# A graph layer on one core: group 0 worked in pairs of tiles, the row table moved to step 3, and five unused matmuls at TensorE's start

## The reference

```
h = relu(layernorm(x))                            # per node
W_rel = einsum('rb,bdf->rdf', w_comp, weight)     # 32 types from 8 bases
agg[type, dst] += h[src] * norm                   # per edge
node = einsum('rnd,rdf->nf', agg, W_rel) + bias + h @ loop_weight
out = x + relu(node)
```

## Time and profile before

| | |
|---|---|
| median of 3 runs | 1015.2 us (1015.01 to 1015.9) |
| the profiled execution | 1015.24 us, its span 1013.5 us |
| TensorE busy | 990.3 us, 98% |
| VectorE busy | 955.0 us, 94% |
| ScalarE busy | 884.6 us, 87% |
| GpSimd busy | 723.8 us, 71% |
| granted TensorE clock, mean | 0.999 |

### The profile page before, as it was taken

One profiled execution on the slowest core, in us unless ns is written; L12 is line 12 of the kernel. 1 busy time (PEld: TensorE's weight loads), 2 busy tenths in 40 slices (PEclk: granted clock), 3 DMA queues, 4 the chain that ended last, 5 costly groups with the idle time before them and its releaser, 6 DMA issues.

```text
span 1013.5 us, 23775 instructions
## 1 busy us (share of the span) xinstructions
PE 990.3 (98%) x4902; PEld 574.4 (57%) x4902; DVE 955.0 (94%) x4366; ACT 884.6 (87%) x3242; POOL 723.8 (71%) x1282
## 2 busy tenths in 40 slices
PE   5899999999999999999999999999999999999996
PEld 2355555555556565656565555555555655555655
DVE  6999999999999999999999999999999999999995
ACT  6898989898888889898989898989898988889884
POOL 6877777777777777777777777777777777777740
PEclk9999999999999999999999999999999999999999
DMA  4556555556556555565565555465655655555544
GB/s 116 145 135 165 149 156 164 156 144 169 143 152 173 140 154 161 152 166 155 143 173 141 154 162 158 138 178 140 168 152 152 166 148 155 159 155 141 156 123 140
DMA packets 178223, 154.47 MB, mean 152 GB/s; under 512 B 17781, under 2 KB 151213, under 8 KB 178077
## 3 DMA queue, kind: packets, MB, share of 16 engines
q1 hardware_dynamic: 157261, 101.40, 35.6%
q0 software_dynamic: 20384, 51.32, 19.7%
q10 hardware_dynamic: 432, 0.22, 0.1%
HBM read 101.31 MB, written 51.56 MB: 151 GB/s over the span
## 4 chain that ended last, share of the span: by engine, by line
PE 93%; DVE 2%; POOL 2%; issue 1%; ACT 1%; DMA 1%; DVEq 0%; ACTq 0%; POOLq 0%
PE y_ps L790 33%; PE y_ps L797 31%; PE win_ps L812 9%; PE win_ps L807 8%; PE hT_ps L876 4%; PE hT_ps L803 4%; PE mix_ps L868 1%; POOL xg L578 1%; DVE sum_a L1019 1%; DVE sum_b L1019 0%; DMA xg<-x,idx 0%; DVE msg L1052 0%; PE y_ps L812 0%; DMA src_all<-src 0%; PE y_ps L807 0%
## 5 line engine op out<-in xcount | busy, mean ns | idle before, releaser
L578 POOL DMA_INDIRECT xg<-x,idx x392 | 382.0, 974 | 73.4 <-issue 34.0
L790 PE MATMUL y_ps<-w_all,hT 128*128 128x512 f32 x784 | 412.3, 608 | 2.9 <-DVE sum_a L1019 2.7
L797 PE MATMUL y_ps<-w_all,hT 128*128 128x512 f32 x784 | 400.3, 592 | 0.0
L523 POOL TENSOR_TENSOR u<-z 128x128 f32<-128x128 f32 x392 | 180.4, 460 | 182.8 <-ACT z L626 178.9
L626 ACT ACTIVATE z<-y_ps,mix 128x128 f32<-128x128 f32 x784 | 244.5, 366 | 44.8 <-PE y_ps L797 37.8
L1019 DVE SCALAR_TENSOR_TENSOR sum_b<-y_ps,mix,sum_b 128x128 f32<-128x128 f32 x784 | 265.8, 339 | 0.0
L797 PEld LDWEIGHTS y_ps<-w_all,hT 128*128 128x128 f32 x784 | 149.1, 190 | 187.9 <-issue 164.0
L790 PEld LDWEIGHTS y_ps<-w_all,hT 128*128 128x128 f32 x784 | 132.3, 189 | 119.1 <-DVE sum_a L1019 60.9
L622 ACT ACTIVATE z<-y_ps,mix 128x128 f32<-128x128 f32 x392 | 140.8, 359 | 63.6 <-issue 44.9
L660 ACT ACTIVATE hw<-xw,shift,nrstd 128x128 f32<-128x128 f32 x391 | 192.6, 494 | 0.4 <-DVE shift L1121 0.4
L1019 DVE SCALAR_TENSOR_TENSOR sum_b<-y_ps,mix,z 128x128 f32<-128x128 f32 x392 | 131.4, 335 | 36.1 <-issue 32.3
(11 more groups left out here) (107 smaller groups left out, 1174.3 us busy)
## 6 DMA issues: line engine op xcount, KB each, us to landing
seg<-msgs SPq DMA_DIRECT2D x391, 104.8 KB
msgs<-msg SPq DMA_DIRECT2D x98, 258.0 KB
xw<-x POOLq DMA_DIRECT2D x97, 256.0 KB
out<-res SPq DMA_DIRECT2D x97, 256.0 KB
xg<-x,idx POOLq DMA_INDIRECT x392
type_bc<-type_rows SPq DMA_DIRECT2D x52, 112.0 KB
w_all<-weight SPq DMA_DIRECT2D x1, 512.0 KB
type_bc<-type_rows SPq DMA_DIRECT2D x4, 80.0 KB
```

Of the source, the lines that this page charges most:

```text
L523: nc.gpsimd.tensor_tensor(u[:, r, :], z[:, r, 0, :], z[:, r, 1, :], ALU.add).then_inc(s_u, 1)
L578: nc.gpsimd.indirect_dma_start(xg[:, q, j, :], None, x, bass.IndirectOffsetOnAxis(ap=idx[:, q, j:j + 1], axis=0)).then_inc(s_gather[q * G ...
L790: nc.tensor.matmul(y_ps[2 * t % 5][:, :, :], hT[:, q, j, :], w_all[:, B // 2:B, :], start=True, stop=True).then_inc(s_y_high, 1)
L797: nc.tensor.matmul(y_ps[(2 * t + 1) % 5][:, :, :], hT[:, q, j, :], w_all[:, 0:B // 2, :], start=True, stop=True).then_inc(s_y, 1)
```

## The change

In group 0 each tile gets its own `neg_mean`; tiles 0 and 1 are transposed and copied to `hT` by themselves (`first_tiles`), and the products of tile 0 stand ahead of the transposes of tiles 2 and 3, those of tile 1 behind them. `w_all` is loaded straight behind the first types, and the rest of `src_all` behind the fourth gather. Of the 8 `sign` instructions four are moved into ScalarE's steps 1 and 2. `bin_counts(0)` moves to the start of VectorE's step 1, `bin_counts(1)` to the start of its step 3 and `row_table` to the end of that step; the 8 matmuls of `count_bins` stand together in TensorE's step 3. Five matmuls 128x384 in float32 into bank `y_ps[4]`, whose result nothing reads, stand ahead of the first mixing matmul.

```diff
+TABLE_STEP = 3
+PAIR = 2
...
@@ SyncE
-            sp.dma_start(src_all[:, FIRST:NT], src[:, FIRST:NT]).then_inc(s_src, 16)
-            sp.wait_ge(s_gather[1], 16)
             sp.dma_start(w_all[:, :, :], weight.rearrange("b d f -> d b f")).then_inc(s_all, 16)
             sp.wait_ge(s_gather[G - 1], 16)
+            sp.dma_start(src_all[:, FIRST:NT], src[:, FIRST:NT]).then_inc(s_src, 16)
@@ ScalarE, step: behind mixing(1) i = 0, behind mixing(3) i = 1
+                def late_sign(i):
+                    if is_before(g, TABLE_STEP):
+                        sign(SPAN // 2 + 2 * (g - 1) + i)
@@ ScalarE, group 0
-            for k in range(SPAN - 2):
+            for k in range(SPAN // 2 - 1):
                 sign(k)
...
+            for j in range(PAIR):
+                act.wait_ge(s_mean_first, j + 1)
+                first_relu(j)
+            act.wait_ge(s_hT_first, 1)
+            nc.scalar.activation(hT[:, 0, 0:PAIR, :], hT_ps[:, 0:PAIR, :], ACT.Copy).then_inc(s_hT_sb_first, 1)
+            sign(SPAN // 2 - 1)
+            act.wait_ge(s_mean_first, PAIR + 1)
+            first_relu(PAIR)
             act.wait_ge(s_mean, 1)
-            first_relu(2)
-            first_relu(3)
+            first_relu(G - 1)
@@ TensorE
+            pe.wait_ge(s_step, 2)
+            for k in range(5):
+                nc.tensor.matmul(y_ps[4][:, 0:3, :], ident[:, :], win_off[:, 0:3 * P], start=True, stop=True)
...
                 messages(0)
                 messages(1)
+                if g == TABLE_STEP:
+                    count_bins()
...
+            def first_tiles():
+                for j in range(PAIR):
+                    pe.wait_ge(s_relu, j + 1)
+                    mm = nc.tensor.transpose(hT_ps[:, j, :], h[:, 0, j, :], ident[:, :])
+                mm.then_inc(s_hT_first, 1)
+                pe.wait_ge(s_hT_sb_first, 1)
+                pe.wait_ge(s_all, 16)
+                product_high(0, 0, 0)
+                product_low(0, 0, 0)
+                for j in range(PAIR, G):
+                    pe.wait_ge(s_relu, j + 1)
+                    mm = nc.tensor.transpose(hT_ps[:, j, :], h[:, 0, j, :], ident[:, :])
+                mm.then_inc(s_hT, 1)
+                product_high(0, 0, 1)
+                product_low(0, 0, 1)
@@ VectorE, step
+                if g == 1:
+                    bin_counts(0)
+                if g == TABLE_STEP:
+                    bin_counts(1)
                 tile_slot(g, n, q, 0, more)
...
                 tile_slot(g, n, q, 3, False)
                 stats_of(3)
+                if g == TABLE_STEP:
+                    row_table()
                 if more:
                     one_hot(g + 1, (q + 1) % RING)
@@ VectorE, group 0
+                dve.wait_ge(done, 2 * (j % DV) + 2)
+                nc.vector.tensor_scalar(neg_mean[:, 0, j:j + 1], nmv[:, NRING - 1, j, 0:1], -1.0, None,
+                                        ALU.mult).then_inc(s_mean_first if j < G - 1 else s_mean, 1)
                 if j == 1:
...
                     one_hot(0, 0)
-                    bin_counts(0)
...
-            bin_counts(1)
             step(0, 0, 0)
-            row_table()
```

More of the change, by code:

```diff
@@ L270, in build_layer @@
         s_mean_first = sem("s_mean_first")
+        s_hT_first = sem("s_hT_first")
+        s_hT_sb_first = sem("s_hT_sb_first")
         s_dst = sem("s_dst")
@@ L627, in scale_bases, with sign @@
                 ins.then_inc(s_z, 1)
+            def sign(k):
+                nc.scalar.activation(signs[:, k, :], dst_f[:, :], ACT.Sign, bias=limits[:, k:k + 1], scale=-1.0,
+                                     accum_out=below_sum[:, k:k + 1]).then_inc(s_below, 1)
             def group_means(g, n, q):
@@ L704, in step @@
                 mixing(1)
+                late_sign(0)
                 if here:
@@ L719, in step @@
                 mixing(3)
+                late_sign(1)
                 if not beyond(g, NG - 1):
@@ L729, in _ @@
             act.wait_ge(s_limits, 1)
[L730 to L732 removed]
             def first_relu(j):
                 nc.scalar.activation(h[:, 0, j, :], xg[:, 0, j, :], ACT.Relu, bias=neg_mean[:, 0, j:j + 1]).then_inc(s_relu, 1)
[L737 removed]
+            for k in range(SPAN // 2 - 1):
                 sign(k)
[L739 to L743, removed]
+            for j in range(PAIR):
[6 more added lines that the diff above has]
+            first_relu(PAIR)
             act.wait_ge(s_mean, 1)
[L745 to L746 removed]
+            first_relu(G - 1)
             nc.scalar.activation(std[:, 0, :], nmv[:, NRING - 1, :, 1], ACT.Sqrt, bias=eps_col[:, 0:1]).then_inc(s_std, 1)
             act.wait_ge(s_hT, 1)
[L749 removed]
+            nc.scalar.activation(hT[:, 0, PAIR:G, :], hT_ps[:, PAIR:G, :], ACT.Copy).then_inc(s_hT_sb, 1)
             group_means(1, 0, 1)
@@ L772, in _, with count_bins @@
         def _(pe):
-            def count_bins(half):
+            def count_bins():
                 counts = win_ps[0:1, :, :].rearrange("p b f -> p (b f)")
                 pe.wait_ge(s_first_hot, 1)
-                pe.wait_ge(s_bins, half + 1)
-                for k in range(half * (SPAN // 2), (half + 1) * (SPAN // 2)):
+                pe.wait_ge(s_bins, 2)
+                for k in range(SPAN):
                     mm = nc.tensor.matmul(counts[:, 0:BINS], in_bin16[:, k:k + 1], first_hot[:, SPAN - k:SPAN - k + BINS],
                                           start=k == 0, stop=k == SPAN - 1)
-                if half == 1:
-                    mm.then_inc(s_hist, 1)
+                mm.then_inc(s_hist, 1)
+            pe.wait_ge(s_step, 2)
+            for k in range(5):
+                nc.tensor.matmul(y_ps[4][:, 0:3, :], ident[:, :], win_off[:, 0:3 * P], start=True, stop=True)
             pe.wait_ge(s_weights, 16)
@@ L840, in messages @@
                 def messages(j):
-                    if 1 <= g <= NG:
-                        if j == 0:
+                    if 1 <= g <= NG and not (is_before(g, 2) and j < PAIR):
+                        if j == (PAIR if is_before(g, 2) else 0):
                             pe.wait_ge(s_hT_sb, g)
-                        if g == 1 and j == 0:
-                            pe.wait_ge(s_all, 16)
                         product_high(g - 1, (q - 1) % RING, j)
@@ L870, in step @@
                     if is_before(g, 1):
-                        count_bins(0)
+                        first_tiles()
+                        return
                     pe.wait_ge(s_relu, g * G + G)
```

6 lines of the change are left out of this document (removed).

## The result

Ten executions of each, taken in turn on one chip: before 1015.62 us (1015.01 to 1016.89), after 1018.44 us (1017.65 to 1020.11). The ratio is 1.0029 with an interval of 1.0020 to 1.0038, some 2.8 us, above the forecast of 1016.8 and just above the range. The profiled execution of after took 1018.74 us with a span of 1017.0 (before 1015.24 and 1013.5).

A forecast was written before the change was run, and what follows sets the result against it. TensorE bounds the full pipeline; GpSimd's first `u` and VectorE from 32 us decide its gap-free start. +2.49 + 0.34 - 1.2 = +1.6 us on a profiled 1015.24, median 1016.8; range 1014.6 to 1018.3.

The forecast's parts named there:

- The table: VectorE's step 3: row table 2.49 us plus `bin_counts(1)` 0.34, taken as the full 2.83 us of cost; bounds 0 and 2.83.
- The first `u`: GpSimd's first `u`, 20.26 us before: expected 1.2 us earlier, bounds 0.34 and 1.48, passed whole to VectorE at 32.26.
- case B: Slower: constant loads in the DMA queue keep group 1's last gather late; 1017.7, or 1019.2 at worst; chance 0.30.
- The bins on TensorE: Eight small matmuls in TensorE's step 3, beside the row table's time: zero, up to 1.46 us if uncovered.
- the signs: Four signs moved into gaps of ScalarE's steps 1 and 2: zero, 0.60 us without that cover.
- the five unused matmuls: TensorE, ahead of the first mixing matmul: can give back 0.90 us of the first product, which has slack: zero.
- The head start of the first products: TensorE's first product near 10.7 us instead of 16.74; TensorE must then wait, any gain read at GpSimd's `u`.
- Case E: Faster: TensorE's products start 6.0 us earlier and GpSimd does not hold that gain back; 1012.0; chance 0.10.
- C: VectorE's lateness in step 3 is made good before TensorE's gaps end, so the table is covered; 1014.0; chance 0.08.
- D: TensorE's first product was on the path and its clock counts: 0.9 less than forecast, 1015.9; chance 0.07.

## Why the prediction was wrong

**The table: right in place and size.** 2.49 and 0.34, together 2.83 us, were to go over whole to the product of tile 14. That product is 2.94 us late with `u` unmoved, and with `u` 1.9 us earlier it is 1.93 us less late. The last matmul moved by 2.84, and the kernel with the table back at the start gives 3.1.

**The first `u`: the step that failed.** The sum took off 1.2 us, "near the upper end, because both parts of that wait are relieved"; its bounds were 0.34 and 1.48. Measured: 0.02 later in the profile of after, and 0.23 and 0.30 earlier (20.03 and 19.96) in two kernels with the same loads, without the unused matmuls and with the gap filled, in which GpSimd began on time. The text looked at one road, ScalarE's: its new loads "are what the last gather of group 1 competes with". That gather did stay late. But the lower bound held GpSimd's gain at 14.89 or better, and in front of the gain stands a gather too, the sixth, issued at 11.27 beside loads issued from 11.13 on. The gain came at 16.12, and at 15.87 and 15.80 in those two kernels. With the constant loads out of its way the reward came: 1.9 us at the first `u`, more than the upper bound. The mechanism is that of case B, which was to decide once `u` came after 19.46; its price of 1017.7 still held 0.34 us of gain, and with that at zero the sum is 1015.2 + 2.83 = 1018.0 (against before's median of ten, 1015.62 + 2.83 = 1018.45, beside 1018.44 measured). That it meets so closely is in part luck: the four executions above 1019 lift the median, and the other six have 1018.06. The Trainium skill (DMA: Bandwidth & Descriptors, Issuing engines are not separate DMA queues) says that transfers of SyncE and GpSimd share the 16 engines; the sixth gather, issued at 10.80 and 10.79 and read at 15.04 with the loads and 13.28 without them, agrees.

**What was costed at nothing.** The bins on TensorE, the signs, `bin_counts(0)`, the five unused matmuls: taking out the last changed nothing. The first three show no cost of their own in after and weren't tried one by one. The kernel with the table alone shows, though, that without pairs the level of the first product counts: its second half took 1.71 us for 0.86, and the first `u` came 0.81 late. That the sums of bins had kept TensorE at the high level for that half is not shown, since with the bins in place it took 1.36 us in the kernel with the unused matmuls alone. In after the pairs give the first `z` enough of a head start to hide this.

**The head start of the first products** was 5.83 us (10.91 for 16.74) and was lost whole: 4.88 us of it stand as a wait of TensorE ahead of the third tile's second half. Case E is out, as are C (tile 14 was late) and D (the first product's clock).

**Outside the prediction: the clock behind the table.** A gap of 2.5 us on TensorE costs 1.6 to 1.7 us more where the granted clock falls. The prediction took the gap as the whole price. What it does to the time of after is open: its profile has the gap at a granted clock of 1.00, and the filled kernel's ratio is 0.0011 lower, with overlapping intervals, without the executions above 1019; 0.3 us of that is its first `u`, at 19.96. That those four are executions in which the clock fell behind the table was not seen in a profile of after itself; it is argued from two profiles of kernels beside it and from the two filled ones. Against it speak the two kernels with the table at the start and norm, `dst_c` and the types behind the fourth gather: they have no such gap (TensorE waits 0.23 us ahead of tile 14), and yet executions at 0.993, 1.5 to 2.5 us above their medians. So clock lost elsewhere, at the start above all, where the profile of after runs at 0.50 for 4.80 us, is a rival that no run excludes.

## What to carry to other kernels

Work that moves costs what its new place costs: 2.8 us of VectorE were free while it waited for the first `z`, and cost 2.8 us among the sums of step 3, where TensorE waited for it. When a load is moved, list every transfer that is under way at its new time and what each feeds; the one that is hurt may be an earlier one than the last. And a gap on the engine that bounds the kernel may cost its clock as well as its length, so look at the length of the next matmuls, and at the spread over executions, not only at the gap.

## What the hardware showed that was not expected

- The granted clock fell to 0.51 behind gaps of 2.48 and 2.49 us on TensorE in two kernels, and stayed at 1.00 behind one of 2.49 us in after. With eight unused matmuls in the gap, 1.95 us of work, it was 1.00 in both profiles, and the spread of eleven executions was 1.02 and 0.41 us, where it was 2.46 (ten) and 2.02 without them.
- A high clock bought with unused matmuls doesn't last, and doesn't always come: with the later loads the first product took 1.87 us to the next start in spite of them. In after the wait of 4.88 us ahead of 20.57 brought it down again. The windows:

```profile
20.50:25.30 4.80, 4.73 (x10) 2.73 (x11) 2.85 (x15) 4.14 (x17) 4.20 (x9) 0.50 0.34 96
25.30:28.00 2.70, 2.70 (x8) 1.18 (x7) 2.70 (x13) 1.89 (x8) 2.50 (x4) 0.97 0.10 29
```

  Five microseconds of products ran at the 1.2 GHz level there, and it cost nothing in this profile, since GpSimd's gathers held the chain; in the profile without the unused matmuls such a stretch cost 0.4 us at the fifth `u`. The Trainium skill (TensorE: Matmul & The Clock Gate, Part 1) calls the throttled state the default, which activity releases; both stretches agree.
- A gather of 128 rows, from the start of its issue to its first read, took 13.29 - 10.81 = 2.48 us without the constant loads beside it and 15.36 - 11.27 = 4.09 us with them. The same gather in other kernels took 2.49 without, and 3.25 to 4.29 with them, so the loads' price varies from one profile to the next.
- GpSimd's first copy of indices took 0.72 to 0.74 us in four of the thirteen profiles and 0.18 to 0.29 in the others, and in those four all gathers of the first two groups were issued about 0.5 us later. It falls on kernels with and without the change; no run explains it.
- VectorE and ScalarE stood still until about 22 us in one profile, though the matmuls they waited for are recorded as done 5 us before. No run here explains it.
